# Weight loads issued one pair of heads later in a decoder layer's first pass: where the loads, their scans and the stores stand in each engine's order

## What is computed

```python
qkv = x @ w_qkv                          # 1024 x 3072 weights, float32
q, k, v = split(qkv, heads=16, dim=64)
attn = softmax(mask(q / 8 @ k.T))        # causal
out = (attn @ v) @ w_out
```

## Time and profile before

| | |
|---|---|
| median of 3 runs | 2649.22 us (2646.92 to 2655.89) |
| the profiled execution | 2649.22 us, span from first to last instruction 2647.3 us |
| TensorE busy | 2398.3 us, 91% |
| VectorE busy | 1847.3 us, 70% |
| ScalarE busy | 817.4 us, 31% |
| GpSimd busy | 711.0 us, 27% |
| mean granted TensorE clock | 0.963 of full |
| DMA queue of SyncE | 391.07 MB, 67.4% of 16 engines' span |

### The profile page before, as it was taken

How to read it: one execution, slowest core, us unless ns; L and a number is a source line. 1 busy time by engine, 2 the same in 40 slices (tenths; PEclk the granted TensorE clock), 3 DMA queues, 4 the chain that set the end, 5 groups by cost and what they waited for, 6 DMA issues and landing times.

```text
span 2647.3 us, 38004 instructions
## 1 busy us (share of the span) xinstructions
PE 2398.3 (91%) x14411; PEld 1174.9 (44%) x14411; DVE 1847.3 (70%) x3423; ACT 817.4 (31%) x1629; POOL 711.0 (27%) x981
## 2 busy tenths in 40 slices
PE   4888998899989999899898999979988999988996
PEld 2334443454444444454453444444444444435444
DVE  5677887557857776756876777765695777765576
ACT  2454333322123333321213333331221333342110
POOL 3333443124212222213402222222430222221220
PEclk9999999899999999899998999989998999999997
DMA  7687878867547777866745777686663677776543
GB/s 213 160 216 166 187 189 180 204 135 151 116 102 146 145 144 146 188 150 145 149 104 126 143 146 142 130 203 155 147 132 94 136 147 144 143 164 169 112 80 96
DMA packets 983130, 393.49 MB, mean 149 GB/s; under 512 B 936796, under 2 KB 946012, under 8 KB 982948
## 3 DMA queue, kind: packets, MB, share of 16 engines
q1 hardware_dynamic: 982948, 391.07, 67.4%
HBM read 122.56 MB, written 33.55 MB: 59 GB/s over the span
## 4 chain that ended last, share of the span: by engine, by line
PE 60%; DVE 19%; DMA 8%; issue 7%; ACT 3%; POOL 3%; SPq 1%; ACTq 0%; POOLq 0%; DVEq 0%
PE ps_p L565 8%; PE ps_p L567 8%; PE ps_p L566 8%; DMA r<-pn 7%; PE ps_s L565 7%; PE ps_s L566 7%; PE ps_s L567 7%; PE ps_s L625 6%; PE ps_o L652 5%; DVE pn L880 4%; DVE peak L920 2%; ACT probs L798 2%; DVE bn L885 2%; PE ps_s L630 1%; POOL pn L1170 1%
## 5 line engine op out<-in xcount | busy, mean ns | idle before, releaser
L1170 POOL TENSOR_SCALAR pn<-probs,rden 128x640 f16<-128x640 f32 (+7 forms) x512 | 394.6, 783 | 1255.2 <-DVE rden L932 752.2
L798 ACT ACTIVATE probs<-ps_s,low,sizes 128x640 f32<-128x640 f32 (+7 forms) x512 | 421.6, 827 | 855.8 <-DVE low L923 746.9
L880 DVE SCALAR_TENSOR_TENSOR pn<-probs,rden,pn 128x640 f16<-128x640 f32 (+7 forms) x512 | 458.9, 933 | 153.2 <-POOL pn L1170 151.8
L565 PE MATMUL ps_p<-r,w 128*128 128x512 f16 x1344 | 515.9, 384 | 1.6 <-DVE qk L880 1.5
L566 PE MATMUL ps_p<-r,w 128*128 128x512 f16 x1344 | 515.3, 383 | 0.0
L567 PE MATMUL ps_p<-r,w 128*128 128x512 f16 x1344 | 514.8, 383 | 0.0
L625 PE MATMUL ps_s<-qk 64*128 64x512 f16 (+3 forms) x2304 | 245.8, 340 | 117.3 <-ACT probs L798 106.4
L920 DVE TENSOR_REDUCE peak<-ps_s 128x2 f32<-128x1280 f32 (+3 forms) x128 | 241.5, 1887 | 88.7 <-PE ps_s L630 86.1
L652 PE MATMUL ps_o<-r,vn 128*64 128x512 f16 (+3 forms) x2304 | 212.6, 341 | 34.8 <-issue 34.8
L625 PEld LDWEIGHTS ps_s<-qk 64*128 64x128 f16 x2304 | 91.8, 97 | 266.1 <-ACT probs L798 140.4
L567 PEld LDWEIGHTS ps_p<-r,w 128*128 128x128 f16 x1344 | 132.9, 99 | 162.6 <-issue 7.1
(11 more groups left out here) (189 smaller groups left out, 3543.0 us busy)
## 6 DMA issues: line engine op xcount, KB each, us to landing
w<-w_pairs SPq DMA_DIRECT2D x72, 512.0 KB, 4.0
r<-wo_pairs SPq DMA_DIRECT2D x16, 1024.0 KB, 6.4
w_raw<-in_x SPq DMA_DIRECT2D x32, 512.0 KB, 4.0
out<-r SPq DMA_DIRECT2D x32, 512.0 KB, 2.9
w_pairs<-w SPq DMA_DIRECT2D x24, 512.0 KB, 5.3
qk<-in_x SPq DMA_DIRECT2D x24, 512.0 KB, 4.5
w_raw<-in_ctx_t SPq DMA_DIRECT2D x16, 512.0 KB, 5.1
w_raw<-in_w_qkv SPq DMA_DIRECT2D x14, 512.0 KB, 6.1
```

The costliest lines, as they stand in the source:

```text
L565: pe.matmul(ps, lh, rh, start=start and k == ks[0], stop=False)
L798: act.activation(probs_part(q, j, w), ps_s[:, j, scores(q)], ACT.Exp, bias=low[:, n % 2, i:i + 1], scale=sc(n), accum_out=den[:, n % 2, i: ...
L880: dve.scalar_tensor_tensor(out=to, in0=bank, scalar=scale, in1=rounded, op0=ALU.mult, op1=ALU.subtract).then_inc(ok, 1)
L1170: pool.tensor_scalar(to, src, scale, 1.0, ALU.mult, ALU.mult).then_inc(ok, 1)
```

## The change

It concerns pairs 0 to 5 of the first batch, in which the raw weights of the pairs 2 to 7 are loaded. Blocks 0 and 1 of a pair were loaded near the end of the pair three before it (`WI0+++`, `WI1+++`, behind `T6`, and for pair 2 in the start list). Now they are loaded in the pair two before it: block 0 as the first step of SyncE's list, ahead of `T0`, and block 1 behind `T1`. Block 2 stays behind `T2`. The steps `WN0++` and `WN1++` on ScalarE stand where they stood; `WN2++` moves ahead, from behind `CH10+` to before `E50`. The store `WS1` moves from behind `T6` to between `T0` and `T1` of the next pair. Twelve `SI`/`SN` steps are spaced alike in pairs 0 and 1: the three last `SN` of each of the two pairs, which stood behind `E71` and behind `E11` and `E21` of the next pair, now stand behind `E61` (one) and behind `E71` (two). `SM` moves ahead from `R3` to `R1` of pair 2. The first load of block 2 into its buffer no longer waits for the block before, which lay elsewhere.

```diff
@@ ACT_BODY, SP_BODY, SP_START
-    E00 E01 CH21 E10 E11 WN0++ E20 E21 CH00+ WN1++ E30 E31 OH1- E40 E41 CH01+ E50 E51 CH10+ WN2++ OH0 E60 E61
+    E00 E01 CH21 E10 E11 WN0++ E20 E21 CH00+ WN1++ E30 E31 OH1- E40 E41 CH01+ WN2++ E50 E51 CH10+ OH0 E60 E61
     CH11+ E70 E71 CH20+
...
-    WD2+ T0 T1 WS2+ WI2++ T2 T3 T4 WD0++ T5 T6 WS0++ WI0+++ WS1++ WI1+++ WD1++ T7 V+
+    WD2+ WI0++ T0 WS1+ T1 WI1++ T2 WS2+ WI2++ T3 T4 WD0++ T5 T6 WS0++ WD1++ T7 V+
...
-    WI2++ WS0+ WS1+ WS2+ WS0++ WI0+++ WS1++ WI1+++ V+
+    WI2++ WS0+ WS1+ WS2+ WS0++ V+
@@ ONCE
-    ("DVE", 2, "R3"): "SM", ("PE", 2, "S5"): "SC1", ("DVE", 2, "X5"): "SC1",
+    ("DVE", 2, "R1"): "SM", ("PE", 2, "S5"): "SC1", ("DVE", 2, "X5"): "SC1",
...
-for pair, at, row in ((0, "T0", (0, 1, 2)), (0, "T4", (3,)), (0, "T5", (4,)), (0, "T6", (5,)),
-                      (1, "T1", (6,)), (1, "T2", (7,)), (1, "T3", (8,)), (1, "T5", (9,)), (1, "T6", (10,)),
-                      (1, "T7", (11,))):
-    ONCE["SP", pair, at] = " ".join(f"SI{e:02d}" for e in row)
-for e, (pair, at) in enumerate([(n, at) for n in (0, 1) for n, at in (
-        (n, "E41"), (n, "E51"), (n, "E61"), (n, "E71"), (n + 1, "E11"), (n + 1, "E21"))]):
-    ONCE["ACT", pair, at] = f"SN{e:02d}"
+for pair, first in ((0, 0), (1, 6)):
+    for at, row in (("T0", (0, 1, 2)), ("T4", (3,)), ("T5", (4,)), ("T6", (5,))):
+        ONCE["SP", pair, at] = " ".join(f"SI{first + e:02d}" for e in row)
+    for at, row in (("E31", (0,)), ("E41", (1,)), ("E51", (2,)), ("E61", (3,)), ("E71", (4, 5))):
+        ONCE["ACT", pair, at] = " ".join(f"SN{first + e:02d}" for e in row)
@@ SyncE, WI
-                        if n >= 2:
+                        if n >= 3 or n == 2 and t < 2:
                             sp.wait_ge(w_ok, 3 * n + t - 2)
```

## The result

The changed kernel takes 2744.97 us (median of 4 runs, 2738.93 to 2747.06) against 2652.55 us (2646.92 to 2662.26) for the kernel before on the same chip: a ratio of 1.034, with a 95% interval of 1.0304 to 1.0378, so 81 to 100 us slower. The prediction said 2747, from 2695 to 2785. The profiled execution of the changed kernel took 2750.7.

What follows compares the result with a forecast made beforehand. A ring of dependent steps, not busy TensorE, was taken to bound the first batch's pairs. Load waits 90.6, pair 0 -5.5, regrouped steps +8.3, clock +9, relief -4 make 98 us: about 2747, range 2695 to 2785.

Steps and rivals of the forecast that it cites:

- The place and the ring: Pairs 0 to 5: dependent steps from one transpose to the next; a delay reaching VectorE lengthens the pair, by 15.1 us.
- signs: Changed profile: three load waits in each of pairs 0 to 5, longest at block 1's; pairs 1 to 5 at 68 to 72 us.
- Pair 3, step by step: Walk through pair 3 in the new order: E31 ends 14.2 us late, whole pair 15.1 longer.
- The waits add up: Three load waits in one ring: 15.1 us per pair, 90.6 over six; +65 to +125 in all had chance 0.73.
- the first wait: ScalarE's block 0 sum of squares waits for its late load: a delay of 9 us, 3 of them covered.
- rival (a): Waits cover each other, one left per pair: 6.7 us a pair, 2697; chance 0.14, including what lies up to the forecast.
- The third wait: ScalarE's block 2 sum, ahead of E50, waits for its load: loses the 3.7 us given back, and 0.9 more, per pair.
- The clock: TensorE idles nearly 15 us per pair, then runs at about half speed: 1.5 us per pair, 9 in all.
- The regrouped steps: Ends of pairs 0 and 1 on ScalarE: a regrouped step behind E71 waits for its load, together 8.3 us.
- The moved store: Block 1's store in SyncE's queue: costs nothing, 0.6 us of queue time in a gap.
- The relief ahead of T7: Fewer loads ahead of that transpose on SyncE, so it lands sooner: 4 us back in all, at best 11.
- Pair 0, pair 1 and the total: Pair 0's first wait nearly covered, 5.5 us off; both pairs' regrouped-step waits 8.3; total about 2747.

Runs made afterwards that it cites:

- E50: Not a run: a step in ScalarE's list, before which the change puts block 2's sum of squares; in pair 3 before, it started at 271.08.
- E71: Not a run: a step late in ScalarE's list for a pair, behind which the change puts two of the regrouped steps.
- E00: Not a run: the first step of ScalarE's list, from which pair lengths are counted; in pair 3 at 242.56 before, 287.87 changed.
- E31: Not a run: a step in ScalarE's list behind block 1's sum of squares; in pair 3 it ended at 257.47 before, 316.12 changed.
- E41: Not a run: a step in ScalarE's list, behind which a regrouped step stood in the kernel before, waiting 0.73 there.
- E40: Not a run: a step in ScalarE's list, ahead of which a regrouped step stands after the change.

## Why the prediction was right, and where its parts were off

**The place and the ring.** Right. The loss lies in pairs 0 to 5, all 18 sums of squares wait for loads, and the ordinary pairs of the later batches are unchanged. That ScalarE's order is the cause of some 69 of the 90 us is shown by the run that moves only the sums of squares. Two of the signs that the prediction named came out otherwise: pairs 1 to 5 were to take 68 to 72 us, and pair 1 took 76.7 and pair 2 66.7; the longest wait was to be WN1's, and in pairs 2 to 5 it is WN0's (9.08 against 7.44 in pair 3). The second is a slip, since the prediction's own walk gives WN0 a wait of 9.05, and WN1 no more than that.

**Pair 3, step by step**, counted from E00. R2 was to move by 6.1 and moved by 6.5 (305.66 less 287.87, against 253.80 less 242.56). T1: 3.75 forecast, 4.2 measured. The loads of blocks 0, 1 and 2: 4.6, 5.0 and 5.8 taken; 5.1, 3.8 and 5.8 measured. End of E31: 14.2 and 13.3. R4: 10.5 and 10.4. E50 after E31's end: 14.5 and 14.4. The whole pair: 15.1, before the clock, and 14.8. The row for a split block behind V was a good stand-in for the load that the trace did not have. The load behind T1 was faster than its stand-in; the queue had stood empty for 3.7 us ahead of that T1, and in the run with block 0 early, directly behind a load, a store and T1, the same load took 5.2.

**"The waits add up."** Right for what matters, too strong as a law. As parts in a row they make the pair's length, but they are not independent prices. The expectation put the first wait at some 4.5 us in a pair, and giving it back gained 7 us in all instead of 22, since T0 waits for M1- and T1 then meets the store and the traffic behind T0. So there was some truth in rival (a): some 19 of 88 us of the two waits are covered. Its own price (2697, or +48) was far off, since it left out the third wait. With it the same steps give 10.4 + 0.9 = 11.3 in a pair and 6 x 11.3 + 8 = 76 in all, against 83 measured with block 0 early.

**The third wait.** Its size is right: E50 came 14.4 us behind E31's end. The wait at WN2 needs two moves together, the load of block 2 behind T2 and WN2 ahead of E50. It is there with both other loads early too (35.1 us in total), but then it mostly lies under a wait that E50 has anyway. Moving WN2 alone costs nothing in the kernel before. No run undoes the third wait in the changed kernel, so the 4.6 us in a pair that the prediction gives it (3.7 and 0.9) are worked out and not measured by themselves.

**The clock.** TensorE idled 13.84 us ahead of S4 (nearly 15 forecast), S4 took 1.78 where the trace of before has 0.99 for the same twelve matmuls, and the granted clock was 0.58 over the 6 us behind it, so mostly 1.2 GHz. R4 stayed on its forecast and E50 0.1 ahead of it, both worked out at full clock, so the 9 us for the clock are not seen in pair 3. T2 was about 0.7 later for it, but took 1.42 and not the 2.60 assumed. That the two cancel is my reading of one pair; no run separates the clock. Over pairs 2 to 5 the terms of the prediction come to 63.7 (15.1 each, and 0.8 for clock and relief together) and the table has 58.9.

**The regrouped steps.** The size was nearly right (8.3 forecast, 10 measured) by luck in part, since the place was half wrong. SN05 is as described. Missed were SN06, which was moved from behind E41 to ahead of E40 and waits there for a load behind M1- (6.4 to 7.3 us in the two versions shown; in the changed kernel it stands behind WN1's wait of 11.2 and shows none), and the 1.8 that pair 2 gains.

**The moved store.** Wrong: it was put at nothing, as 0.6 us in a gap. By itself it costs 5 us (1 to 9). It stands ahead of T1, and T1 frees the buffer for H30; in pair 3 of that run L30 waits 1.8 longer. In the changed kernel T1 is late anyway, so it should hardly count there; the run that takes it back (5 less, with overlapping intervals) does not show whether it does.

**The relief ahead of T7.** The size was right. T7 of pairs 0 to 5 landed 8.5, 7.8, 7.6, 6.7, 7.3 and 6.7 us after its issue in the kernel before and 7.0, 6.9, 6.8, 6.7, 6.7 and 6.7 in the changed one, 3.8 less in all where the term took 4. What of it reaches the time is not measured. The bound of 11 was never near, since no T7 that was read landed in under 6.6.

**Pair 0, pair 1 and the total.** 12.5 and 20.9 against 14.6 and 20.1 by the prediction's terms (15.1 each, 5.5 off in pair 0, 4.15 for an SN wait, 0.8 for clock and relief together). In pair 1 the three SI loads stand ahead of block 1's, and WN1 waits 11.2 there instead of 7.4. Pair 6, which has none of these loads, is 1.8 longer, and nothing was forecast for it. So the sum of 98 and the 94 of the table agree more closely than their parts do: pairs 0 and 2 to 5 come out 6.9 below their terms, pairs 1 and 6 2.6 above.

**What stays open.** With later sums and the old spacing, 14 us are left while the store explains some 5. The rest may lie with block 1's load between T1 and T2 or with block 2's store and load behind T2: it is gone when both are moved forward and the store WS1 behind T1, but they were not moved one by one. In the same way the 21 us with both loads early are the regrouping (10), the store (5), WN2's move (1) and some 5 for which block 2's place behind T2 is the one remaining part, not run by itself; the intervals of these runs are as wide as that rest. No version tried beats the kernel before.

## What to carry to other kernels

A load is late relative to its first reader's place in that reader's queue, so when a load moves, move its reader, or look up what stands behind the reader: here a sum of squares held up the exponentials, though its result is not needed for some 25 us (in pair 3 of the kernel before WN1 ran at 251.57, and the scale stands behind X6, which ran at 274.75). In a ring of dependent steps, price each part by walking the ring once with all parts in it, and do not price a single part as its share of that sum: alone, the first wait was worth a third of what its step showed. A long idle time ahead of a step is not its price either: WN2 waited 35 us in all where the pairs grew by little, because the step behind it was not due. Look as well at what shares a queue with a transfer of the ring: a store of 0.6 us of queue time ahead of T1 cost 5 us (1 to 9). And compare a changed list step by step: block 2's load had changed sides of T2, and the run that moved only its reader could not show what the two moves do together.

## What the runs showed of the hardware

The 512 KB loads that read `w_qkv` landed in 3.7 to 7.3 us in pairs 0 to 6 of the changed kernel, median 4.6, and WI1 in 3.8 in pair 3, behind one transposing DMA with little else under way. The estimate of 3.2 by the Trainium skill (DMA: Bandwidth & Descriptors, Anatomy of one DMA — SWDGE (gpsimd) path), whose fit is for DMAs issued from GpSimd while these are issued from SyncE, was not reached by any. A transposing DMA's time in SyncE's queue depends on what stands ahead. T1, 1024 columns of float16, took 1.23 behind an empty queue (changed kernel, pair 3) and 1.23 to 1.26 directly behind one load (kernel before, pairs 3 to 5). It took 1.45 and 1.47 directly behind one store (the moved store alone, pairs 1 and 2), and 2.07 and 2.12 behind a load and a store (pairs 3 and 5 of the same run, and 2.07 with block 0 early), though 1.60 in pair 4 of the first of these runs, where the store itself took 1.28. In pair 3 T1 landed 4.5 us after its issue behind the load and 5.8 behind the load and the store.
